# Softmax reciprocals turned once and spread by DMA, partial contexts loaded four heads at a time, their product on GpSimd

## What is computed

```
x   = LN(src) * (1 + scale) + shift              # scale, shift from the timestep
q, k, v = heads of x @ Wq + bq, x @ Wk + bk, x @ Wv + bv
s   = q k^T / sqrt(32) + attention_bias          # bias: (2, 16, 2048, 2048) float32
s   = where(src_mask, -inf, s)
ctx = softmax(s) v                               # (2, 2048, 512)
x   = x + (ctx @ Wo + bo)
h   = LN(x) * g2 + beta2
u   = h @ W1 + b1                                # d_ff = 2048
x   = x + (u * sigmoid(1.702 u)) @ W2 + b2
out = pairs (x0,x1) and (x2,x3) of x rotated by theta, phi
```

## Time and profile before

| | us |
|---|---|
| median of three runs | 3511.86 (3510.07 to 3513.74) |
| the profiled execution | 3513.55 |
| its span | 3511.9 |
| TensorE busy | 3415.5 (97%) |
| VectorE busy | 2484.8 (71%) |
| ScalarE busy | 1885.7 (54%) |
| GpSimd busy | 2084.0 (59%) |

### The profile page before, as it was taken

The page is one execution under the profiler, slowest core; times in us unless marked ns, Lnnn a source line. Parts: engine busy times, 40 slices in busy tenths (PEclk is TensorE's granted clock), DMA queues, the critical chain, the costliest instruction groups (busy, mean ns, idle before and its releaser), DMA issues.

```text
span 3511.9 us, 60955 instructions
## 1 busy us (share of the span) xinstructions
PE 3415.5 (97%) x18338; PEld 1940.6 (55%) x18338; DVE 2484.8 (71%) x4176; ACT 1885.7 (54%) x2541; POOL 2084.0 (59%) x646
## 2 busy tenths in 40 slices
PE   8999799999999999999999999998899999999997
PEld 3444466666666666666666666665344444444443
DVE  5666599999999999999999999997333343342331
ACT  3222388888888888888888888885111111111110
POOL 0000499999899999999998999995211211220100
PEclk9999899999999999999999999999999999999999
DMA  8999999999999999999999999999311220220100
GB/s 286 340 339 339 359 364 349 346 346 353 396 345 344 352 351 348 394 349 350 348 350 366 375 351 345 349 348 325 83 35 38 72 55 17 72 67 4 48 12 12
DMA packets 288702, 906.20 MB, mean 258 GB/s; under 512 B 93344, under 2 KB 93344, under 8 KB 211360
## 3 DMA queue, kind: packets, MB, share of 16 engines
q1 hardware_dynamic: 240272, 811.43, 64.3%
q10 hardware_dynamic: 45840, 86.00, 6.9%
q0 software_dynamic: 2560, 8.39, 0.6%
HBM read 763.12 MB, written 142.61 MB: 258 GB/s over the span
## 4 chain that ended last, share of the span: by engine, by line
PE 85%; DVE 1%; DMA 1%; issue 0%; ACT 0%; SPq 0%; POOL 0%; DVEq 0%; ACTq 0%
PE b_T L765 27%; PE bank_ctx L788 14%; PE scores L731 14%; PE scores L1302 13%; PE b_T L1312 9%; PE bank_ctx L1312 3%; PE scores L1283 3%; PE scores L737 1%; DMA penb<-in_L_cond_b 1%; PE scores L1243 0%; PE scores L1292 0%; DVE probT L1150 0%; PE scores L1257 0%; ACT penb L1048 0%; DVE stats_c L1141 0%
## 5 line engine op out<-in xcount | busy, mean ns | idle before, releaser
L590 POOL TENSOR_TENSOR ring<-ring,penb 128x1856 f32<-128x1856 f32 x512 | 1903.9, 3756 | 504.1 <-DMA penb<-pen_scratch 418.4
L685 ACT ACTIVATE ring<-ring,low 128x2048 f32<-128x2048 f32 x512 | 1029.0, 2010 | 317.9 <-DVE low L654 317.9
L765 PEld LDWEIGHTS b_T<-ident,ring 128*128 128x128 f32 x8192 | 889.7, 141 | 432.7 <-DVE probT L638 429.5
L765 PE MATMUL b_T<-ident,ring 128*128 128x128 f32 x8192 | 1091.2, 276 | 5.2 <-DVE probT L638 4.5
L654 DVE CUSTOM_DVE_ANT_0 ring<-scores,ring 128x1024 f32<-128x1024 f32 x512 | 627.2, 1225 | 177.0 <-PE scores L731 154.1
L638 DVE COPY probT<-b_T 128x512 f32<-128x512 f32 x1024 | 702.1, 686 | 3.9 <-PE b_T L765 3.8
L654 DVE CUSTOM_DVE_ANT_0 ring<-scores,ring,low_part 128x1024 f32<-128x1024 f32 x512 | 652.6, 1275 | 0.4
L731 PE MATMUL scores<-keys,queries 128*128 (+1 forms) x2048 | 620.8, 424 | 21.3 <-DMA queries<-q_rows 16.9
L788 PE MATMUL bank_ctx<-probT,values 128*32 128x512 f32 x4096 | 545.3, 605 | 0.2 <-ACT ctxp L701 0.2
L695 ACT COPY probT<-b_T 128x512 f32<-128x512 f32 x1024 | 537.8, 575 | 0.5 <-PE b_T L765 0.5
L1015 POOL TENSOR_TENSOR keys_again<-keys_again,values 128x512 f32<-128x512 f32 x32 | 40.4, 1264 | 787.4 <-DVE values L1232 787.4
(11 more groups left out here) (127 smaller groups left out, 1912.2 us busy)
## 6 DMA issues: line engine op xcount, KB each, us to landing
ring<-in_fside_Bx16xSxS SPq DMA_DIRECT2D x512, 1024.0 KB, 7.5
keys<-k_rows SPq DMA_DIRECT2D x64, 1024.0 KB, 8.4
values<-v_heads ACTq DMA_DIRECT2D x128, 256.0 KB, 6.3
queries<-q_rows SPq DMA_DIRECT2D x128, 256.0 KB, 8.0
ctx_scratch<-ctxp ACTq DMA_DIRECT2D x128, 256.0 KB, 6.6
penb<-ctx_scratch SPq DMA_DIRECT2D x120, 256.0 KB, 4.7
k_rows<-part_hi SPq DMA_DIRECT2D x64, 256.0 KB, 3.3
k_rows<-part_lo SPq DMA_DIRECT2D x64, 256.0 KB, 3.4
```

Of the source, the lines that this page charges most:

```text
L590: nc.gpsimd.tensor_tensor(ring[:, j, 0:POOL_MASKED], ring[:, j, 0:POOL_MASKED], penb[:, j, 0:POOL_MASKED], ALU.add).then_inc(masked, 1)
L685: nc.scalar.activation(ring[:, k, :], ring[:, k, :], ACT.Exp, bias=low[:, k:k + 1], scale=-1.0, accum_out=column(sums_all, trip, k)).then_ ...
L765: last = nc.tensor.transpose(turn_bank(slot, n)[:, c * P:(c + 1) * P], ring[:, slot, at:at + P], ident[:])
```

## The change

- The reciprocals of a whole group (128 columns) are turned by one transpose, four in all. `divisors` now works on groups: group 0 before the last trip's closing steps, the other three in one go behind them. `keep_rows` copies the turned reciprocals into `low_all` and stores them in a new DRAM tensor `recip_scratch`, one row of 1024 queries for each head and group.
- `load_per_row` reads them back: for four heads one transfer that repeats each head's 512 reciprocals on 32 partitions. `widen` and the 16 transposes of each supertile are gone.
- The store of `ctxp` puts quarter g of dimension d at row 4 d + g. `load_parts` then takes four heads in one transfer with 8 KB in a row.
- The product of reciprocals and contexts moves from VectorE's `front` to GpSimd (`context`) for all supertiles but the first. GpSimd starts it for the second when `first_hn` is complete.
- In the first front `bo` is loaded early with a semaphore of its own, the additions of `bo` stand ahead of the products, and the wait for the other vectors stands behind them. W2's first quarter is loaded last, since its place holds reciprocals for the first supertile.

The diff, cut to its core:

```diff
@@ phase_b, scalar @@
-                act.dma_start(ctx_scratch[bass.ds((trip // H) * 2 * H + hh * H + trip % H, 1)].rearrange("o p n -> (o p) n"),
+                act.dma_start(ctx_scratch[bass.ds((trip // H) * 2 * H + hh * H + trip % H, 1)].rearrange("o (d g) q -> (o g) d q", g=4),
                               ctxp[:]).then_inc(ctx_stored, 16)
@@ phase_c @@
+    first_per_row = [per_row[:, 0], per_row[:, 1], ring[:, 4, 0:TOK], ring[:, 4, TOK:2 * TOK]]
+    recip_rows, undefined = up
+    GROUPS = TRIPS // H
+    GC = H * R
+    def of_groups(all_tiles, first, count):
+        return all_tiles[:, first * H:(first + count) * H, :].rearrange("p t r -> p (t r)")
@@ sync @@
         def load_parts(to, v, c, signal):
-            for k in range(4):
-                sp.dma_start(to[DH * k:DH * (k + 1)],
-                             ctx_scratch[bass.ds(v * H + 4 * c + k, 1)].rearrange("o (g d) q -> d (o g) q", d=DH)).then_inc(signal, 16)
+            sp.dma_start(to.rearrange("p k n -> p (k n)"),
+                         ctx_scratch[bass.ds(v * H + 4 * c, 4)].rearrange("h (d g) q -> (h d) (g q)", g=4)).then_inc(signal, 16)
+        def load_per_row(to, group, half, c, signal):
+            sp.dma_start(to, recip_scratch[bass.ds(group * H + 4 * c, 4), bass.ds(half * TOK, TOK)]
+                         .rearrange("h (o n) -> h o n", o=1).to_broadcast([4, DH, TOK])).then_inc(signal, 16)
...
-        sp.dma_start(g2_all, row(g2)).then_inc(vec_in, 16)
+        sp.dma_start(bo_all, row(bo)).then_inc(bo_in, 16)
...
         after_scores(7)
+        sp.dma_start(b2_all, row(b2)).then_inc(vec_in, 16)
+        sp.dma_start(g2_all, row(g2)).then_inc(vec_in, 16)
         sp.dma_start(beta2_all, row(beta2)).then_inc(vec_in, 16)
-        sp.dma_start(bo_all, row(bo)).then_inc(vec_in, 16)
-        sp.dma_start(b2_all, row(b2)).then_inc(vec_in, 16)
-        for c in range(4):
+        after_turns(4)
+        sp.wait_ge(recip_stored[0], 16)
+        for c in range(DB):
+            load_per_row(first_per_row[c], 0, 0, c, per_row_ld)
+        for c in range(1, 4):
             after_turns(4 + c)
             load_w2(c)
         for c in range(2):
             sp.wait_ge(ctxT_ready, 3 + c)
             load_w1(c)
+        load_w2(0)
...
                 load_parts(parts[:, c % 2], v, c, part_ld[c % 2])
+                load_per_row(per_row[:, c % 2], v // 2, v % 2, c, part_ld[c % 2])
@@ gpsimd @@
+        def context(v, c):
+            pool.wait_ge(part_ld[c % 2], (v - 1) * 64 + (c // 2) * 32 + 32)
             add_parts(parts[:, c % 2], v, c)
+            pool.wait_ge(summed, v * DB + c + 1)
+            if c == 0:
+                pool.wait_ge(wo_done, v * QT)
+            nc.gpsimd.tensor_tensor(ctxT[:, c, :], parts[:, c % 2, 0, :], per_row[:, c % 2], ALU.mult).then_inc(ctxT_ready, 1)
...
+        pool.wait_ge(first_hn, QT)
         for c in range(DB):
-            parts_of(1, c)
+            context(1, c)
@@ scalar @@
-    def widen(act, v, c):
+    def keep_rows(act, first, count, n):
+        act.wait_ge(recip_turned, n)
+        nc.scalar.copy(of_groups(low_all, first, count), recip_rows[:, first * GC:(first + count) * GC]).then_inc(recip_copied, 1)
+        act.wait_ge(recip_copied, n)
+        act.dma_start(recip_scratch[first * H:(first + count) * H, :].rearrange("(g h) (j q) -> (h j) g q", h=H, q=P),
+                      of_groups(low_all, first, count).rearrange("p (g q) -> p g q", q=P)).then_inc(recip_stored[n - 1], 16)
@@ vector @@
+    def divisors(dve, first, count, n):
+        cols = slice(first * GC, (first + count) * GC)
+        sums = of_groups(sums_all, first, count)
+        nc.vector.tensor_scalar(undefined[:, cols], of_groups(low_all, first, count), 2.0, 0.0, ALU.mult, ALU.mult)
+        nc.vector.reciprocal(sums, sums).then_inc(recip_chain, 1)
...
-            dve.wait_ge(left.pv_done, left.PV0 + 2 * TRIPS - 1)
-            context(0)
-            context(1)
-            dve.wait_ge(vec_in, 80)
+            dve.wait_ge(left.exp_done, TRIPS * R)
+            divisors(dve, 1, GROUPS - 1, 2)
+            dve.wait_ge(bo_in, 16)
             dve.wait_ge(xm_ld, 16)
-            for t in range(2):
+            for t in range(QT):
                 last = nc.vector.tensor_tensor(xm_in[:, t, :], xm_in[:, t, :], bo_all, ALU.add)
             link(last)
+            dve.wait_ge(left.pv_done, left.PV0 + 2 * TRIPS - 1)
+            dve.wait_ge(per_row_ld, DB * 16)
+            for c in range(DB):
+                context(c)
+            dve.wait_ge(vec_in, 64)
...
             if 1 <= f <= DB:
-                c = f - 1
-                dve.wait_ge(summed, v * DB + c + 1)
-                dve.wait_ge(recip_turned, v * DB + c + 1)
-                nc.vector.tensor_tensor(ctxT[:, c, :], fore[c % 2], parts[:, c % 2, 0, :], ALU.mult).then_inc(ctxT_ready, 1)
@@ tensor @@
-    def turn_recip(pe, v, c, bank):
-        for t in range(QT):
-            last = nc.tensor.transpose(bank[:, t * P:(t + 1) * P], recip_wide[:, c % 2, t, :], ident[:])
+    def turn_recip(pe, first, count, n):
+        pe.wait_ge(recip_ready, n)
+        for g in range(first, first + count):
+            last = nc.tensor.transpose(recip_rows[:, g * GC:(g + 1) * GC], of_groups(sums_all, g, 1), ident[:])
         last.then_inc(recip_turned, 1)
...
         pe.sem_inc(down_done, 4)
+        turn_recip(pe, 1, GROUPS - 1, 2)
```

More of the change, by code:

```diff
@@ L610, in trips @@
                 step(it, j)
+        after(-1)
         for j in range(R):
@@ L834, in phase_c @@
     xm_in = places(penb, 4, 2).rearrange("p (t n) -> p t n", n=D)
-    recip_wide = places(penb, 6, 1).rearrange("p (a t n) -> p a t n", a=2, n=P)
-    bo_all, b2_all = places(penb, 7, 1)[:, 0:D], places(penb, 7, 1)[:, D:2 * D]
-    g2_all, beta2_all = (f32(left.queries[:, i, :]) for i in range(2))
+    per_row = places(penb, 6, 1).rearrange("p (a n) -> p a n", n=TOK)
+    g2_all, beta2_all = places(penb, 7, 1)[:, 0:D], places(penb, 7, 1)[:, D:2 * D]
+    bo_all, b2_all = (left.queries[:, i, :] for i in range(2))
     first_parts = [parts[:, 0], parts[:, 1]] + [ring[:, i, :].rearrange("p (k n) -> p k n", n=TOK) for i in range(2)]
+    first_per_row = [per_row[:, 0], per_row[:, 1], ring[:, 4, 0:TOK], ring[:, 4, TOK:2 * TOK]]
     early, late_half = (left.probT[:, i].rearrange("p k n -> p (k n)") for i in range(2))
@@ L875, in phase_c @@
     summed = sem("summed")
+    recip_chain = sem("recip_chain")
     recip_ready = sem("recip_ready")
-    wide_ready = sem("wide_ready")
     recip_turned = sem("recip_turned")
+    recip_copied = sem("recip_copied")
+    recip_stored = [sem(f"recip_stored{i}") for i in range(2)]
     ctxT_ready = sem("ctxT_ready")
@@ L1042, in gpsimd @@
             pool.wait_ge(y_stored[i], NU * QT // 2 * 16)
[L1044 to L1049 removed]
+    def keep_rows(act, first, count, n):
[4 more added lines that the diff above has]
+                      of_groups(low_all, first, count).rearrange("p (g q) -> p g q", q=P)).then_inc(recip_stored[n - 1], 16)
     def scalar_between(act, j):
         if j == 0:
[L1054 to L1058 removed]
+            keep_rows(act, 0, 1, 1)
     def scalar(act):
+        keep_rows(act, 1, GROUPS - 1, 2)
         for t in range(QT):
@@ L1068, in front @@
         def front(v, f):
-            if 1 <= f <= DB:
-                widen(act, v, f - 1)
             if f == 10:
@@ L1159, in front @@
             x2_v = of(x2, v)
-            if f == 0:
-                need(dve, wide_ready, v * DB)
-                divisors(dve, v)
-                need(dve, wo_done, v * QT)
-            if 1 <= f <= DB:
-                c = f - 1
-                dve.wait_ge(summed, v * DB + c + 1)
-                dve.wait_ge(recip_turned, v * DB + c + 1)
-                nc.vector.tensor_tensor(ctxT[:, c, :], fore[c % 2], parts[:, c % 2, 0, :], ALU.mult).then_inc(ctxT_ready, 1)
             if f == 4:
@@ L1173, in front @@
                     last = nc.vector.tensor_tensor(xm_in[:, t, :], xm_in[:, t, :], bo_all, ALU.add)
-                link(last, 2)
+                link(last, 1)
             if 5 <= f < 9:
@@ L1183, in front @@
                     last = nc.vector.bn_stats(stats[:, t, :], x2_v[:, t, :])
-                link(last, 3)
+                link(last, 2)
                 dve.nop(nofuse=True)
@@ L1194, in front @@
                     last = nc.vector.tensor_scalar(hn[:, t, :], x2_v[:, t, :], mean_var[:, t, 0:1], rstd[:, t:t + 1], ALU.subtract, ALU.mult)
-                link(last, 5)
+                link(last, 4)
             if f == 11:
@@ L1198, in front @@
                     last = nc.vector.tensor_tensor(hn[:, t, :], hn[:, t, :], g2_all, ALU.mult)
-                link(last, 6)
+                link(last, 5)
                 for t in range(QT):
@@ L1267, in front @@
         def front(v, f):
-            if 1 <= f <= DB:
-                c = f - 1
-                pe.wait_ge(wide_ready, v * DB + c + 1)
-                if c < 2:
-                    need(pe, hT_ready, v * DB - 1 + c)
```

(6 more changed lines are left out.)

78 lines of the change are left out of this document (28 added, 50 removed).

## The result

The changed kernel takes 3551.60 us (median of four runs, 3548.03 to 3554.02) where the kernel before takes 3512.59 beside it: a ratio of 1.0110 with an interval of 1.0097 to 1.0122. It is slower by 39 us, where the prediction said faster by 16. The span of the profiled execution is 3551.0 us.

The account below looks back on a forecast made before the run. TensorE's own work was taken as the bound, 85% of the chain that ended last. From 3511.9 us, -23 (final stage), +2 (turn), -1 (to the FFN) and +6 (attention) gave 3496 us, range 3480 to 3514.

Parts of the forecast that it names:

- The final stage: Seven supertiles lose 16 transposes each and the first turn's wait on TensorE, 3.3 us per supertile: -23 us.
- From Wo to the FFN: VectorE's last four additions before the first FFN product are less held up by GpSimd sums: -1 us (0 to -3).
- Four engines: The new `ctxp` store and `per_row` loads, outer run 4, use four DMA engines, not 16; about two chances in three.
- The turn, +2: Between attention and final stage, reciprocals go through DRAM and back on four engines, so Wo starts at 2449: +2 us.
- Attention, +6: Where groups of heads begin, four engines carry the store's extra bytes and delay ring loads: +6 us (0 to +12).
- Rival C: In attention the four engines cannot carry their load: slower, 3545 us halfway, up to 3640 by share; chance 0.13.
- Rival B: The store and the loads use all 16 engines, with Wo 6 us earlier: 3482 us; chance 0.22.
- Rival D: Reciprocals' DRAM round trip 8 us later, or GpSimd's fourth context 1 us late in each supertile: 3504 us; chance 0.15.

Follow-up runs that it names:

- x_two: The changed kernel with two `ctxp` buffers, one for each half of a trip, store still on four engines: 3511.9 us, 0.9997 of the kernel before.
- x_store16: The changed kernel with the store of `ctxp` cut into four transfers of 32 rows, 16 engines each: 3518.1 us, 1.0014 of the kernel before.
- x_old: The changed kernel with `ctxp` store and `load_parts` as before the change, and `per_row` loads in four transfers on 16 engines: 3491.4 us, 0.9941 of before.
- x_two_row16: x_two with the `per_row` loads cut into four transfers on 16 engines: 3501.2 us, 0.9964 of the kernel before.
- runs of 4: Not a follow-up run or kernel: transfers whose outermost dimension has length 4, which used four DMA engines; no time of its own.
- x_late_w1: x_old with two quarters of W1 loaded behind the reciprocals instead of ahead of them: 3485.4 us, 0.9919 of the kernel before.

## Why the prediction was wrong, by its own steps

**The final stage: right.** -23 was worked out, -23.6 measured, and the distance between supertiles came out at 125.35 us against 125.3. GpSimd's products stayed under TensorE: in the 129 us from 2738 TensorE is busy for all 129.

**From Wo to the FFN: right.** -1 against -1.2.

**Four engines: right,** by the packet counts and by the semaphore updates.

**The turn, +2: right in its chain, mis-sized.** +11.8 was measured. The order of events was as told: reciprocals into DRAM, back, contexts. Two terms were too small. The store of the reciprocals was put at 4 us (bounds 2 and 6.3; no row had the lower one) and took 8.0; in the nine other kernels that have it, it took 5.6 to 11.2. The loads were put at 15 us from the first issue at 2431 to the last landing at 2446, which counts each of the four engines as if it worked for them alone; they took from 2486.1 to 2507.9, 21.8 us. Together 4 + 7 = 11 us of error, less 1 since the store was issued earlier than thought.

**Attention, +6: the step that failed.** +53.3 was measured, in two parts. The part that was priced is what four engines cost where groups begin: 12.9 of the 13.4 us that x_two loses, for +6 with bounds of 0 and 12. The place was right, and it cost twice as much: the loads of a beginning delay two trips, not a single tile whose slack of 2 us could be set against them. That the four engines were full there was not shown engine by engine; x_store16, with the same bytes on 16, loses 2.7. The part that was not priced is 40 us, the difference between after and x_two. The prediction took the store for a matter of rates, and asked who reads its data, namely the last stage, much later. It did not ask what the landing frees. `ctxp` is single, ScalarE waits for `ctx_stored` ahead of every copy, and the allowance of 12.5 us between an issue and the next copy could have been read from the trace of before, beside the 6.3 us of the earlier trace rows. A store that puts four times the bytes on each of its engines had 6.2 us of slack to lose.

**Rival C** put 3545 us on the slower side and a chance of 0.13, close to the 3551.6 measured, and it was refuted all the same: with a second buffer the same four engines carry attention at 348 GB/s without a gap. That its time was close is luck, twice over. The reason was another one, and its sum doesn't come out: by bytes the four engines need 29.9 us for a trip (24.7 / 26.2 of 31.7), by the share 34.1 (1.075 of it), and halfway is 32.0 and not 32.5, which makes 0.3 us a trip, +18 and 3514. Rival B's 16 engines are nearest in x_old, though with the old rows for the partial contexts: its 3482 stand against 3491.4 measured, the difference being mostly the turn, where it had Wo 6 us earlier than before and the trace shows it 3 us later (28.3 for 25.2). With the new rows, in x_two_row16, Wo comes 25.7 us after the last addition, still no earlier than before. Rival D's late round trip did come, 10 us instead of 8, on top.

What stays open is why a store on four engines needs 12 to 16 us in the first place. Its own packets would occupy an engine for 2.7 us (32 of 84 ns). The rest it spends among other transfers, on which the runs say little: smaller packets of bias cut the 95% point by 3.0 us and the median by 0.5, and leaving out the transfers of values cut them by 0.9 and 0.2. Which transfers stand in its way these runs don't say.

## What to carry to other kernels

A layout that makes one transfer of four, or its rows longer, may also set how many engines carry it: look at the outermost run of both sides. Runs of 32 and 128 used 16 engines here, and runs of 4 used four. When a transfer gets slower, look not only for who reads what it brings but for who waits to overwrite what it takes away; read from the trace how many microseconds lie between its issue and that wait, and compare. Of the 53.3 us a second buffer brought back 39.9 and four transfers in place of one 26.6, the rest of which went into issuing them; here the best was to leave the store as it was (x_old, x_late_w1).

## What the runs showed of the hardware

A store of 256 KB on four engines beside traffic of 337 GB/s lands in 12.1 us (95%: 15.8; in x_two, at 348 GB/s, 13.1 and 14.8), on 16 engines in 6.6 (8.3) at 346. Four loads of 256 KB that repeat rows of 2 KB take 16.8 to 25.4 us from the first issue to the last landing when each is on four engines (six kernels), and 9.2 to 12.4 when cut for 16 (four kernels). A store of 64 KB in rows of 512 B, on 16 engines, took 5.6 to 11.2 us at the end of attention, in ten kernels. The issue of the store in three dimensions takes ScalarE 0.57 us, in two 0.36, in four pieces 1.8. Four additions of 128x512 on VectorE with both inputs in SBUF take 2.49 us by themselves and 6.77 when GpSimd's sums start with them (x_late_w1, x_old).
